# A merged light and routing stage: nine descent rounds, a search in six groups, 128-lane one-hots, and the first heavy gather issued inside

## What is computed

```
light_out = feed_forward(x, light_*)            # 512 -> 256 -> 512, exact gelu, every token
s = einsum('bnd,d->bn', x, routing_token)
scores = coor_descent(s, k=576, n_iters=50, eps=1)
   # step: a = logk - logsumexp(s + b);  b = -relu(s + a)
sel_scores, sel_idx = top_k(scores, 512)
routed_out = feed_forward(x[sel_idx], heavy_*)  # 512 -> 2048 -> 512
out = x + light_out + scatter(routed_out at sel_idx)
```

## Time and profile before

| | |
|---|---|
| median of 3 runs | 3608.41 us (3606.89 to 3615.33) |
| profiled execution | 3608.13 us, span 3606.4 us |
| granted TensorE clock, mean | 0.956 |
| busy over the span | TensorE 3282.0 (91%), VectorE 2782.5 (77%), ScalarE 1559.9 (43%), GpSimd 1961.1 (54%) |
| `mixed_phase`, first to last | 2913.5 to 3215.2 us |
| first gelu of group 0, 1, 7, 10, 11, 15 | 2937.5, 2953.4, 3044.8, 3103.8, 3119.8, 3197.0 us |
| `heavy_phase` | from 3215.2 us; its first product 3233.1, its last ends at 3589.4 |

### The profile page before, as it was taken

The page is one execution under the profiler, slowest core; times in us unless marked ns, Lnnn a source line. Parts: engine busy times, 40 slices in busy tenths (PEclk is TensorE's granted clock), DMA queues, the critical chain, the costliest instruction groups (busy, mean ns, idle before and its releaser), DMA issues. The chain is left out here.

```text
span 3606.4 us, 55255 instructions
## 1 busy us (share of the span) xinstructions
PE 3282.0 (91%) x16960; PEld 2522.1 (70%) x16960; DVE 2782.5 (77%) x5530; ACT 1559.9 (43%) x5385; POOL 1961.1 (54%) x1819
## 2 busy tenths in 40 slices
PE   5899999999859999999999599999999858879998
PEld 3677777777637777777777477777777646558886
DVE  3788788888677777777775488899899768767775
ACT  0666666666421111111111477777777634211111
POOL 1555555556445666666666466666666623223333
PEclk8899999999979999999999799999999979989999
DMA  6346354454365666666665436545455347520111
GB/s 194 94 132 170 114 151 138 123 169 119 115 197 142 171 157 156 168 162 162 158 158 116 125 110 170 149 111 170 141 144 144 113 164 272 191 94 13 25 23 24
DMA packets 284693, 491.10 MB, mean 136 GB/s; under 512 B 53922, under 2 KB 74722, under 8 KB 283682
## 3 DMA queue, kind: packets, MB, share of 16 engines
q1 hardware_dynamic: 243986, 409.40, 37.4%
q0 software_dynamic: 32256, 77.65, 11.4%
q10 hardware_dynamic: 8208, 1.05, 0.2%
HBM read 250.32 MB, written 136.96 MB: 107 GB/s over the span
## 5 line engine op out<-in xcount | busy, mean ns | idle before, releaser
L835 ACT ACTIVATE t_pr<-ps,t_negmax 128x154 f32<-128x154 f32 x2048 | 869.4, 552 | 367.9 <-DVE t_negmax L617 367.5
L549 POOL TENSOR_TENSOR t_pr<-t_pr,t_inv 128x616 f32<-128x616 f32 x512 | 640.1, 1250 | 575.0 <-DVE t_inv L632 571.9
L835 ACT ACTIVATION_READ_ACCUMULATOR t_pr<-ps,t_negmax 128x1 f32 x2048 | 482.7, 236 | 0.0
L640 DVE COPY t_pTm<-ps 128x512 f32<-128x512 f32 x512 | 349.9, 683 | 166.2 <-PE ps L905 165.4
L617 DVE TENSOR_REDUCE t_negmax<-ps 128x4 f32<-128x616 f32 x512 | 403.4, 788 | 58.1 <-PE ps L892 57.2
L904 PEld LDWEIGHTS ps<-ident,t_pr 128*128 128x128 f32 x2048 | 316.8, 206 | 132.7 <-issue 76.0
L892 PE MATMUL ps<-t_kst,t_stack 98*128 98x154 f32 x2048 | 356.8, 294 | 56.9 <-issue 34.8
L904 PE MATMUL ps<-ident,t_pr 128*128 128x128 f32 x2048 | 344.5, 292 | 18.2 <-DVE t_pTm L640 9.6
L892 PEld LDWEIGHTS ps<-t_kst,t_stack 98*128 98x128 f32 x2048 | 283.2, 196 | 72.0 <-issue 56.4
L74 PE MATMUL ps<-e_xT_high,e_wgu_high 128*128 128x512 f32 x768 | 306.1, 399 | 1.6 <-DVE e_xT_low L1396 1.6
L76 PE MATMUL ps<-e_xT_high,e_wgu_low 128*128 128x512 f32 x768 | 304.8, 397 | 0.0
(11 more groups left out here) (336 smaller groups left out, 8337.7 us busy)
## 6 DMA issues: line engine op xcount, KB each, us to landing
t_stack<-t_q_high SPq DMA_DIRECT2D x1024, 64.0 KB, 2.0
c_wgu_in<-in_gate_upT SPq DMA_DIRECT2D x32, 1536.0 KB, 12.3
t_stack<-t_q_low SPq DMA_DIRECT2D x512, 64.0 KB, 2.0
x_dram<-t_xs SPq DMA_DIRECT2D x32, 1024.0 KB, 6.6
c_wd_in<-in_downT SPq DMA_DIRECT2D x32, 768.0 KB, 13.7
xs_dram<-t_z SPq DMA_DIRECT2D x16, 1032.0 KB, 7.7
l_z<-xs_dram SPq DMA_DIRECT2D x16, 1032.0 KB
t_x<-in_x SPq DMA_DIRECT2D x16, 1024.0 KB
```

What stands on the lines that cost most here:

```text
L549: pool.tensor_tensor(p, p, inv[:, v, :].unsqueeze(1).to_broadcast([P, KEYS, HG]), ALU.mult).then_inc(s["normed"], 1)
L640: dve.tensor_copy(pTm[:, g % 2, :, t * P:(t + 1) * P], ps[:, 4, :].rearrange("p (h n) -> p h n", h=HG)).then_inc(s["pTm"], 1)
L835: op = act.activation(pr[:, u % 4, :, h], flat[:, col:col + KEYS], ACT.Exp, bias=negmax[:, u, h:h + 1], accum_out=total[:, u, h:h + 1])
```

## The change

- The descent takes nine rounds, four of six steps and five of five, in groups 0 to 8. `paces` has new numbers throughout.
- The threshold, its tail and the one-hots take groups 9 to 14.
- The position is split into a tile number (0 to 3) and a lane (0 to 127). `past`, `tile_hot` and `tile_no` are small instructions; `spread` multiplies the values by the tile's one-hot (two instructions of 128x1024 elements); the one-hot has 128 lanes and is made for 8 columns at a time (8 instructions of 128x1024).
- TensorE finds all rows in one go in group 15, between inner products and transposes: 64 matmuls with the one-hot as weights (128 columns) and 32 moving columns. The result has its rows on the right lanes, so the copy of `found` and its transposes are gone.
- `vals` is made by GpSimd before its loop.
- SyncE loads w1 and gamma first, then z, then the rest. VectorE waits for w1 and gamma only, ScalarE for nothing before its copies; the split of w2 moves behind the first seven instructions of the chain, and TensorE waits for it after the inner products of group 0.
- GpSimd issues the four gathers of the first batch inside `mixed_phase`, when `heavy_rows` is ready, into a buffer that is kept for both blocks; `heavy_phase` leaves them out.

```diff
-    ROUND, CLIP = 7, 20.0
-    ROUNDS = (ITERS - 1) // ROUND
+    SIZES, CLIP = (6, 6, 6, 6, 5, 5, 5, 5, 5), 20.0
+    ROUNDS = len(SIZES)
...
-    RING = 14
+    PART = 8
...
-        slots = sb("slots", [P, ROUTED])
-        hot = sb("hot", [P, RING, ROUTED], BF16)
+        past, tile_hot, tile_no = sb("past", [P, C, CC + 1]), sb("tile_hot", [P, C, CC], BF16), sb("tile_no", [P, C])
+        hot = sb("hot", [P, C, P], BF16)
...
-            sp.dma_start(z[0][:], rows(scr["xs"], 0)).then_inc(s["z_in0"], 16)
-            sp.dma_start(w1_in[:], a["light_w1"].rearrange("(k p) n -> p k n", p=P)).then_inc(s["w_in"], 16)
+            sp.dma_start(w1_in[:], a["light_w1"].rearrange("(k p) n -> p k n", p=P)).then_inc(s["w1_in"], 16)
             with nc.allow_non_contiguous_dma(reason="biases by partition"):
-                sp.dma_start(gam[:], a["light_gamma"].rearrange("(k p) -> p k", p=P)).then_inc(s["w_in"], 16)
+                sp.dma_start(gam[:], a["light_gamma"].rearrange("(k p) -> p k", p=P)).then_inc(s["w1_in"], 16)
+                sp.dma_start(z[0][:], rows(scr["xs"], 0)).then_inc(s["z_in0"], 16)
...
+            each = batch[:].unsqueeze(1).to_broadcast([P, C, B])
+            made(pool.tensor_tensor(vals[:, :, 0:B], each, row[:].unsqueeze(2).to_broadcast([P, C, B]), ALU.mult))
+            made(pool.tensor_tensor(vals[:, :, B:2 * B], each, col[:].unsqueeze(2).to_broadcast([P, C, B]), ALU.mult))
...
+            pool.wait_ge(s["xb2"], TG * NG)
+            pool.wait_ge(s["rowed"], 1)
+            for n in range(CC):
+                pool.indirect_dma_start(
+                    out=c["xh0"][:, n, :], out_offset=None, in_=scr["xs"][:, :],
+                    in_offset=bass.IndirectOffsetOnAxis(ap=c["heavy_rows"][:, 0, n:n + 1], axis=0),
+                ).then_inc(c["xh0_in"], 16)
...
+                link(dve.tensor_tensor(past[:], pos[:].unsqueeze(2).to_broadcast([P, C, CC + 1]),
+                                       tile_edge[:].unsqueeze(1).to_broadcast([P, C, CC + 1]), ALU.is_ge))
...
+                link(dve.tensor_tensor(tile_hot[:], past[:, :, 0:CC], past[:, :, 1:CC + 1], ALU.subtract))
...
+                link(dve.tensor_reduce(tile_no[:], past[:, :, 1:CC], AX, ALU.add))
...
+                link(dve.scalar_tensor_tensor(pos[:], tile_no[:], -float(P), pos[:], ALU.mult, ALU.add))
...
+                for half in range(2):
+                    r = slice(half * C // 2, (half + 1) * C // 2)
+                    dve.tensor_tensor(spread[:, r], vals[:, r].unsqueeze(3).to_broadcast([P, C // 2, 2 * B, CC]),
+                                      tile_hot[:, r].unsqueeze(2).to_broadcast([P, C // 2, 2 * B, CC]),
+                                      ALU.mult).then_inc(s["spread"], 1)
...
-                for j in range(C):
-                    reached(dve, s["hot_mm"], j - RING + 1)
-                    dve.tensor_scalar(hot[:, j % RING, :], slots[:], pos[:, j:j + 1], None,
+                for j in range(0, C, PART):
+                    dve.tensor_tensor(hot[:, j:j + PART, :], lane[:].unsqueeze(1).to_broadcast([P, PART, P]),
+                                      pos[:, j:j + PART].unsqueeze(2).to_broadcast([P, PART, P]),
                                       ALU.is_equal).then_inc(s["hot"], 1)
...
-                dve.wait_ge(s["hot_mm"], C)
-                dve.tensor_copy(found[:], ps[0:2 * B, SIDE, :]).then_inc(s["found"], 1)
-                dve.wait_ge(s["found_mm"], 1)
+                dve.wait_ge(s["hot_mm"], 1)
...
-            dve.wait_ge(s["w_in"], W_IN)
+            dve.wait_ge(s["w1_in"], 32)
...
             advance(4 + 3)
+            dve.wait_ge(s["w_in"], W_IN)
+            high_of(dve, w2[0][:], w2_in[:]).then_inc(s["w_high"], 1)
...
                 if n < ROUNDS:
-                    return (13, 7, 2, 2, 2, 1, 1, 0, 0, 4 if n + 1 < ROUNDS else 1)
-                if n < 11:
-                    return (11, 5, 2, 2, 2, 2, 2, 1, 1, 2) if n < 10 else (9, 4, 2, 2, 2, 1, 1, 1, 0, 1)
-                return (4, 2, 1, 1, 1, 1, 1, 1, 1, 0) if n < NG - 1 else (4, 2, 1, 1, 1, 1, 1, 1, 0, 0)
+                    last = 4 if n + 1 < ROUNDS else 1
+                    return (9, 6, 2, 2, 2, 1, 1, 1, 0, last) if SIZES[n] == 6 else (7, 5, 2, 2, 1, 1, 1, 1, 0, last)
+                if n < FOUND_AT - 1:
+                    return 7, 4, 2, 2, 2, 1, 1, 1, 1, 1
+                if n < FOUND_AT:
+                    return 4, 3, 1, 1, 1, 1, 1, 1, 1, 1
+                return 0, 0, 0, 0, 0, 0, 0, 0, 0, 1 if n == FOUND_AT else 0
...
+            def found_rows():
+                pe.wait_ge(s["spread"], 2)
+                for j in range(C):
+                    if j % PART == 0:
+                        pe.wait_ge(s["hot"], j // PART + 1)
+                    mm = pe.matmul(ps[:, SIDE, 0:2 * B * CC], hot[:, j, :], spread[:, j].rearrange("p w n -> p (w n)"),
+                                   start=(j == 0), stop=(j == C - 1))
+                mm.then_inc(s["hot_mm"], 1)
...
                 inner(n, 1)
+                if n == 0:
+                    pe.wait_ge(s["w_low"], 2)
+                if n == FOUND_AT:
+                    found_rows()
...
-            gather(0, range(CC))
             low(0)
             low(1)
```

More of the change, by code:

```diff
@@ L1790, in routing @@
                     dve.wait_ge(s["exped"], 2 * i + 2)
-                    for n in range(ROUND):
+                    for n in range(SIZES[i]):
                         linked()
@@ L1794, in routing @@
                         yield
-                        yield from over_rows(part[:], cap[:], 1.0 / EFF_K, "step" if n + 1 < ROUND else "capped")
+                        yield from over_rows(part[:], cap[:], 1.0 / EFF_K, "step" if n + 1 < SIZES[i] else "capped")
                     dve.wait_ge(s["logged"], i + 1)
@@ L2055, in outer @@
                     mm.then_inc(s["y_mm"], 1)
-            def found_rows(first, last):
-                for j in range(first, last):
-                    pe.wait_ge(s["hot"], j + 1)
-                    pe.matmul(ps[0:2 * B, SIDE, :], vals[:, j, :], hot[:, j % RING, :], start=(j == 0),
-                              stop=(j == C - 1)).then_inc(s["hot_mm"], 1)
+            def found_rows():
[6 more added lines that the diff above has]
+                mm.then_inc(s["hot_mm"], 1)
             for k in range(DC):
                 z_turn(0, k)
-            pe.wait_ge(s["w_low"], 2)
+            pe.wait_ge(s["w_low"], 1)
             for n in range(NG):
@@ L2109, in sb @@
             return ctx.enter_context(nc.sbuf_tensor(f"h_{name}", shape, dt))
-        xh = [sb(f"xh{q}", [P, CC, XS]) for q in range(2)]
+        xh = [c["xh0"], sb("xh1", [P, CC, XS])]
         xg = sb("xg", [P, CAP])
```

63 lines of the change are left out of this document (32 added, 31 removed).

## The result

| | before | after |
|---|---|---|
| median | 3607.65 us (6 runs, 3605.16 to 3615.33) | 3592.64 us (6 runs, 3589.94 to 3598.97) |
| ratio | | 0.995, 95% interval 0.994 to 0.996 |
| profiled execution, span | 3608.13, 3606.4 us | 3595.67, 3594.0 us |

The kernel is faster by 15.0 us where 31.6 were forecast: the side is right, the size is half, and 3592.64 lies above the range (3565 to 3588). The profiled execution of the changed kernel was the second slowest of its six, so its terms lean to the slow side.

A forecast was written before the change was run, and what follows sets the result against it. TensorE bounds the heavy stage; a light turn lasts until VectorE reaches the first result tile, plus 2.9 us. Gains 7.0 + 24.3 - 3.9 - 1.2 + 5.4 = 31.6 take 3608.1 to 3576.5 us, range 3565 to 3588.

The forecast's parts named there:

- three signs of being wrong: Descent turns remaining above 15.2 us, group 14 passing 23 us, or the heavy product waiting on a DMA.
- Turns of the descent: Light stage, turns 1 to 8: fewer steps a turn give three turns of 14.85 us and five of 14.55.
- The rival of VectorE's count: Light-stage turns: each dropped instruction is saved in full, 10.3 us more gain, 3566 us; chance 0.16.
- turns which don't follow the chain: Rival: TensorE and ScalarE handing over set turns; descent stays at 15.25 us, search turns at 17.5; 3585 us, chance 0.16.
- Turns of the threshold and one-hots: Light-stage groups 9 to 14: 16.6 us for groups 9 to 12, 15.6 for 13, 20.0 for 14.
- The clock stood only as a rival: TensorE falls to 1.2 GHz in group 14 and threshold turns, 11 us a turn, up to 3620 us; chance 0.02.
- Group 14: Turn of the one-hots: eight of 128x1024 at 1.2 us each, turn 20.0 us, ends 16 and 26.
- The start: Light-stage start and first turn: w1 first, first product 6.8 us sooner; gain 7.0 us, ends 3 and 8.5.
- The last group: Group 15: 64 row-finding matmuls at 0.1 us replace twelve of 512 columns; cost 3.9 us.
- The end: End of light stage: GpSimd's gathers end 5 us after the last tile, barrier adds 1.6; cost 1.2 us.
- the gather isn't really moved out of the way: Rival: descriptors come after the last row numbers, heavy stage finds its rows as late as before; 3582 us, chance 0.07.
- The joint case: Several of the last three rivals at once with contended one-hots, 4.9 + 3.6 + 8.4 + 6, 3599 us; chance 0.03.

The follow-up runs named there:

- the same again: The changed kernel run once more without any edit; median 3588.85 us, ratio 0.9948.
- E2: Changed kernel with the VectorE piece making row numbers moved in group 15 from result tile 3 to ahead of tile 0; median 3583.21 us, ratio 0.9927.
- E5: Changed kernel with the old stage start: z loaded first, all inputs waited for, w2 split next to w1; median 3590.62 us, ratio 0.9949.
- E1: Changed kernel with extra TensorE matmuls that nobody reads in the stops of groups 9 to 14; median 3579.23 us, ratio 0.9914.
- E6: Kernel before the change with 12 extra matmuls nobody reads in each of groups 7 to 10; median 3604.07 us of 11, ratio 0.9991.
- E9: Changed kernel with GpSimd's bias add in the last group cut to 4 of 512 columns, result incomplete; executed once, 3581.22 us.
- E4: Changed kernel with the first batch's four gathers back at the start of the heavy stage; median 3590.11 us, ratio 0.9952.
- E7: Changed kernel with E1, E2 and the light w2 split moved from VectorE to ScalarE and GpSimd; median 3580.56 us, ratio 0.9922.
- E10: Changed kernel with E1 and E2 together, w2 split left on VectorE; median 3582.13 us, ratio 0.9928.

## Why the prediction was half right

Two steps failed: the sum carried no clock, and the start was taken to keep what it won. Turns 9 to 14 were to gain 11.2 us and gained 0.6 in the first profile and 8.1 in the second; the stage up to the gelu of group 1 was to gain 7.0 and gained 0.2 and 1.5. Of the three signs of being wrong, one came: group 14 passed 23 (23.32 and 23.15). Descent turns stayed below 15.2 on average, and the heavy product didn't wait on a DMA.

**Turns of the descent: right in kind, over-sized.** "So a step less wins only that 0.4": eight turns took 119.25 us, 119.2 to 119.3 in each profile with the new light stage, against 117.3. Of the 11.2 us gained, 10.1 are in turns 7 and 8, which were search turns before. The six that were descent turns already took 91.4 us before, and 90.4 and 89.7 in the two profiles of the changed kernel: dropping steps won 1.1 to 1.7 us, where 3 x 0.4 + 3 x 0.7 = 3.3 were forecast. The rival of VectorE's count would have given 117.3 - 3 x 0.65 - 5 x 0.95 = 110.6, that of turns which don't follow the chain 122.0.

**Turns of the threshold and one-hots: the first failed step.** The sum of these turns carried no clock at all, although showed 0.91 in the stretches whose turns and stops were most like them. The clock stood only as a rival, all or nothing: 11 us a turn, chance 0.02. It is neither. In a turn with a stop of 1.1 to 2.8 us the clock may be at its lower level for a few microseconds, which made turns 0.7 to 2.6 us longer, in some executions and not in others. Five of six turns had that in the first profile, one in the second. Over the six profiles of light stages without fillers or other changes in these turns (after, the same again, E2 to E5) the six turns took 108.0 us on average, over the four with fillers 103.7. With the clock held (E1) the six take 102.7 against 102.0 forecast. The argument used against the rival, that turns of 19.7 us "lost only 9%" of their clock, was itself the price that belonged in the sum: E6 has it as 2.0 us of such a turn.

**Group 14.** 20.0 was forecast; it is 21.3 at full clock with fillers, and 22.7 to 23.7 without. One-hots contended at 1.51 on average instead of 1.2 account for 2.4 us of VectorE's time; E9 puts 1.2 to 1.3 us of the turn on them, against the two profiles of the changed kernel. The range knew this: its end for contended one-hots was 6 us.

**The start: the second failed step.** Three numbers failed. z landed 5.3 us into the stage before and 8.7 now (7.5 to 8.9 over the ten profiles with the new start), so w1 and gamma ahead of it cost 3.3 us (2.2 to 3.6) and not 1.4; 1.4 us pass before z's load is issued at all. The scores, which were to "still land at about 2926", 12.5 us into the stage, landed at 14.3 (12.7 to 14.3). And the w2 split was put "beside 24 matmuls at the half clock (0.43 us apart, 10 us)", but from 2929.76 on they were 0.23 us apart, so all 24 took 5.8 us (7.2 to 7.5 in E1, E4, E7, E9 and E10, where the first of them ran at 0.43), and behind the split stood the chain. The path had a term missing besides: TensorE, done sooner with group 0's inner products, then stood still before group 1's transposes, most likely for a z that SyncE had issued no sooner than before. E5 shows the size of it all: its first product is 6 us later than after's, and its gelu 1 only 0.6.

**The last group: mis-sized in our favour.** The 64 row matmuls, reckoned at 0.1 us each, took 1.76 us together, 0.027 each, below the low end of 0.03, which turns a cost of 3.9 into a gain of 0.7; the other 0.7 of the 1.4 seen isn't accounted for. The rule of the Trainium skill (TensorE: Matmul & The Clock Gate, LDWEIGHTS) that was weighed there, 107 ns for a load of 128 columns, is contradicted by the same line: 1.76 us for 64 of them with their matmuls. The same page of the Trainium skill (TensorE: Matmul & The Clock Gate, Weight-path perf modes — Fast Weight Load (FWL) and DoubleRow) has loads of 128 columns that are not float32 go faster than that; this agrees in direction, and no run here took such loads with another width to test it. The prediction says that no row of before has 128 bf16 columns. Its trace has 128 such loads in the expert stage (L1538, 65 rows), eight of them with matmuls of 132 columns in 1.06 us, but at 0.12 us a pair they would not have ruled the 107 ns out.

**The end: a landing was left out.** The prediction ended the gathers with GpSimd's last issue, "5 us after that tile", and added the barrier. The stage ends only when they have landed. GpSimd's issue ended 5.1 us after the tile as forecast, the last gather landed 3.0 us after that, and the stage began 1.1 us later. What the heavy start gained (5.1, forecast 5.4, right) the end took back but for 1.1 us (E4). That is close to the rival "the gather isn't really moved out of the way", chance 0.07, by another road: the rows are there in time, but the barrier waits for them.

**The range.** It names ends for the start (-4 and +1.5 us of gain), the one-hots (-6 and +4) and the row finding (-8.4 and +4.5). Added up they reach from 3566.5 to 3594.9, which holds 3592.64; the 3570 to 3584 given doesn't follow from them by any rule that is stated. The joint case also counts 4.9 us for descent turns where the rival has 1.2 + 3.5 = 4.7.

**What stays open.** Why the same stop lets the clock fall in one execution and not in the next. Where the timed gain of E1 over the change (0.9914 against 0.9948 and 0.995, 12 to 13 us) sits: the profiles give the fillers 4.3 us of turns 9 to 14 on average, and E1's whole stage is as long as that of the same kernel again (296.4 and 296.3), whose start was 2.5 us shorter; only one or two executions of each kernel were profiled. What makes turn 0 some 3 us longer in three of seven profiles: a fall like group 9's, 3.6 us at 0.43 instead of 0.23, loses 1.7 of them. And whether the z of group 0 could keep its old landing with w1 ahead.

## What to carry to other kernels

Where the profile of before shows a granted clock below 1.00 in stretches with stops of one to three microseconds, that loss belongs in the sum of every new turn with such stops, as a range from nothing to a sixth of the turn (here 2.6 us of 15.1), and a few matmuls that nobody reads, placed in the stop, are a cheap test and here also the better kernel. An earlier first product is worth little if setup work is moved into the turn behind it and if that turn's next input is issued no sooner. Work that is issued before a barrier to hide its latency must have landed, not only been issued, before the work that the barrier already waited for.

## What the runs showed of the hardware

- 64 pairs of a weight load (128x128 bf16) and a matmul of 32 columns took 1.76 us, 0.027 each.
- With a stop of 2.12 us before the same matmul in the same kernel the turn's mean clock was 1.00 in one execution (turn of 16.10) and 0.90 in another (17.48).
- In this kernel a stage's end waits for the landing of gathers that GpSimd issued in it: in thirteen profiles the next stage's first instruction came 1.08 to 1.13 us after the later of the last store's and the last gather's landing, whether that was 4.2, 5.7 or 8.1 us after the last result tile.
- Eight 128x1024 one-hots with two SBUF inputs took 1.21 or 1.22 us each without GpSimd's add beside them (E9), and 1.51 on average with it, 2.21 at most.
